# Value products behind the neighbour pieces in each attention slot

## The chip, the core and the metric

The kernel runs on one core of one Trainium2 chip. The metric is device time in microseconds (us) of one execution. The core's engines are named as in the profile: PE is TensorE, which multiplies; PEld is its loading of weights; DVE is VectorE; ACT is ScalarE; POOL is GpSimd; SP issues transfers. Each engine works through its own queue in order, and they wait for each other with semaphores.

## What is computed

The input is 8 batches of 256 tokens of width 512, in 32-bit floats. Four layers follow each other, each as `x = x + layernorm(layer(layernorm(x)))`: a state-space mixer with an MLP, a LoRA MLP, an attention layer, and a linear layer with table-coded weights. The change lies in the attention layer, which the kernel fuses with the last one:

```
qkv = x @ w_qkv                                  # 32 query heads, 8 key/value heads of width 16
xq, xk = rope(xq), rope(xk)
scores = where(causal, xq @ xk.T * scale, -inf)  # per head, 256 x 256
out = softmax(scores) @ values                   # values repeated over 4 query heads
y = out @ w_o
...
x = x + layernorm(y)
x = x + layernorm(layernorm(x) @ w.T + bias)     # the last layer
```

## The kernel before, in words

`attention_layer` walks through the 8 batches in slots, 24 to a batch (`UNITS`). A slot belongs to one unit of attention: a key/value head g and a part r, where r = 0 is the first 128 query rows of four query heads and r = 1, 2 are the second 128 rows of two heads each. The work of a unit is spread over several slots, and every engine has its own loop over the slots:

- `scores(u)` on PE (L1762 to L1769): query times key, then the mask as one more product with an identity matrix. It is issued one slot ahead.
- `maximum(u)` on DVE (L1695): the negated row maximum of the scores, `t_nmax`.
- `exponentials(u)` on ACT (L1573): the probabilities `t_p`.
- `transposes(u)` on PE (L1776): four transposes of the probabilities.
- `high(u)` on ACT (L1566) and `low(u)` on DVE (L1701) take the transposed probabilities out of PSUM as two halves, `t_pT_hi` and `t_pT_lo`, whose sum has the full precision.
- `values(u)` on PE (L1791, L1792 for r = 0; L1797, L1798 for r = 1, 2): values times the two halves, into `OT`. It is issued two slots late, and waits for `pl`, that is for `low(u)`.

Beside this, each slot carries pieces of the neighbouring batches, written out by hand in `JOBS_AT`: the turn of the normalised input (`x`, `a`, `h`: four PE transposes, L1830), the projections (`qq`, `kv`, `o`, `l`: products through the helper `product`, L115 to L117), the stacked transposes that make the query and key tiles (`q`, `k`, L1843), and the transposes of the finished attention output (`back`, L1836). They share two PSUM banks in turn, and `bank_read` waits until the piece that had the bank before has been read out.

What the other engines do for the pieces stands at fixed places of their loops. In its slot s, DVE first drains the pieces that PE ended in slot s - 1 (`drain`), then takes `maximum(s + 1)`, then `turned_low` (L1687), which makes `t_hT_lo`, the low half of a turned input, then `low(s - 1)`, then the statistics of the layernorms. ACT drains the pieces first (`t_hT_hi` L1513, `t_qT` L1523, `t_kT` L1528, `t_v` L1534, `t_oT` L1561), then `high(s - 1)`, then `exponentials(s + 1)`. POOL makes the stacks two slots ahead (L1430, L1432).

A projection needs both halves of its turned input. Below, slot numbers are those within a batch. In four places a piece follows the slot in which its input, or the input that had its bank, was turned: slot 7 (`qq` after `x` in slot 6), slot 10 (`o`, whose bank the turn `a` of slot 9 had), slot 19 (`l` after `h` in slot 18) and slot 22 (`l` after `h` in slot 21). The table lines of these:

```
    (("qq", 0, 1, 1),),                      # slot 7
    (("back", 0, 0, 0), ("o", 0, 0, -1)),    # slot 10
    (("back", 1, 0, 0), ("l", 0, 0, -1)),    # slot 19
    (("l", 0, 1, -1),),                      # slot 22
```

Of the kernel before, what the change touches and what calls it, by code (L numbers as in the profile page):

```python
# [112 lines left out]
def product(pe, out, w_hi, w_lo, x_hi, x_lo, first, last):  # L113

    pe.matmul(out, w_hi, x_hi, start=first, stop=False)  # L115
    pe.matmul(out, w_hi, x_lo, start=False, stop=False)  # L116
    return pe.matmul(out, w_lo, x_hi, start=False, stop=last)  # L117
# [1111 lines left out]
SLOTS = BATCH * UNITS  # L1229
# [34 lines left out]
def name_of(what, part, tile, batch):  # L1264

    return (what, tile, batch) if what in HALVED else (what, part, tile, batch)
# [40 lines left out]
def attention_layer(nc, d, consts, stream, w_hi, w_lo, l_hi, l_lo, bias, keep):  # L1307
# [10 lines left out]
    with ExitStack() as ctx:  # L1318
# [48 lines left out]
        def wait(eng, sem, value):  # L1367
            if value > 0:
                eng.wait_ge(sem, value)
# [10 lines left out]
        def bank_of(job):  # L1380
            return ps[:, X + BANK_OF[job], :]
# [367 lines left out]
        def _(pe):  # L1749
            def scores(u):  # L1750
                b, g, r = u // UNITS, u % UNITS // 3, u % 3
                wait(pe, ex, u - 1)
                if u % UNITS == 0:
                    pe.wait_ge(st_out, max(STACKED["q", 0, 1, b], STACKED["k", 0, 1, b]))
                elif u % 6 == 0:
                    pe.wait_ge(st_out, STACKED["q", g // 2, 1, b])
                    if g == 4:
                        pe.wait_ge(st_out, STACKED["k", 1, 1, b])
                bank = ps[:, S + u % 2, :]
                if r == 0:  # L1760
                    for h in range(2):
                        pe.matmul(bank[:, 2 * h * P:2 * (h + 1) * P].rearrange("p (h t) -> p h t", h=2),  # L1762
                                  qT[:, 2 * g + h, 0:P], kT[:, :, g, 0:P], start=h == 0, stop=False)
                    pe.matmul(bank.rearrange("p (h t) -> p h t", h=4), id_r[:, :],  # L1764
                              mask[:, :].unsqueeze(1).broadcast_to([P, 4, P]), start=False, stop=True).then_inc(sc, 1)
                else:
                    pe.matmul(bank.rearrange("p (h t) -> p h t", h=2), qT[:, 2 * g + r - 1, P:SEQ], kT[:, :, g, :],
                              start=True, stop=False)
                    pe.matmul(bank.rearrange("p (h t) -> p h t", h=2)[:, :, P:SEQ], id_r[:, :],  # L1769
                              mask[:, :].unsqueeze(1).broadcast_to([P, 2, P]), start=False, stop=True).then_inc(sc, 1)  # L1770
# [8 lines left out]
            def values(u):  # L1779
                b, g, r = u // UNITS, u % UNITS // 3, u % 3  # L1780
                part, j = g // 3, g % 3
                s = min(r, 1)
                pe.wait_ge(pl, u + 1)
                if u % UNITS == 0:
                    pe.wait_ge(vl, 2 * b + 2)
                fresh, final = j == 0 and r < 2, j == TRIPLES[part][1] - 1 and r != 1
                if fresh:
                    wait(pe, oe[s], 3 * b + part)
                v = lambda t: v2[:, b % 2, t, g * V_STEP - j * HD:g * V_STEP - j * HD + P]
                if r == 0:  # L1790
                    pe.matmul(ps[:, OT, :], v(0), pT_hi[:, u % 2, :], start=fresh, stop=False)  # L1791
                    mm = pe.matmul(ps[:, OT, :], v(0), pT_lo[:, u % 2, :], start=False, stop=final)  # L1792
                else:
                    out = ps[:, OT + 1, (r - 1) * SEQ:r * SEQ].rearrange("p (h n) -> p h n", h=2)
                    of = lambda part, t: part[:, u % 2, :].rearrange("p (h t n) -> p h t n", h=2, t=2)[:, :, t, :]
                    for t in range(2):
                        pe.matmul(out, v(t), of(pT_hi, t), start=fresh and t == 0, stop=False)  # L1797
                        mm = pe.matmul(out, v(t), of(pT_lo, t), start=False, stop=final and t == 1)  # L1798
                mm.then_inc(pv, 1)

            def bank_read(job):

                if job is None:
                    return
                what, t, b = job[0], job[-2], job[-1]
                i = tile(t, b)
                if what in ("x", "a", "h"):
                    pe.wait_ge(tl, TURN[what, t, b] + 1)
                elif what in ("q", "k"):
                    pe.wait_ge(st_out, STACKED[job])  # L1810
                elif what == "back":
                    pe.wait_ge(osm, BACK[job[1], t, b] + 1)
                elif what == "qq":
                    pe.wait_ge(straight, 2 * i + 1)
                elif what == "kv":
                    pe.wait_ge(vl, i + 1)
                elif what == "o":
                    pe.wait_ge(y_out, i + 1)
                elif what == "l":
                    pe.wait_ge(y_biased, i + 1)  # L1820

            def turn(what, t, b, bank):
                if what == "a":
                    pe.wait_ge(on, BACK[2, t, b] + 1)
                    src = ao[:, t, :]
                else:
                    pe.wait_ge(xn if what == "x" else hn, tile(t, b) + 1)
                    src = xf[:, t, :]
                for k in range(DT):
                    mm = pe.transpose(bank[:, k * P:(k + 1) * P], src[:, k * P:(k + 1) * P], ident)  # L1830
                mm.then_inc(x_mm, 1)

            def back(part, s, b, bank):
                pe.wait_ge(oe[s], 3 * b + part + 1)
                for h in range(4):
                    mm = pe.transpose(bank[:, h * P:(h + 1) * P], oT[:, s, h * P:(h + 1) * P], ident)  # L1836
                mm.then_inc(x_mm, 1)

            def stack(what, part, t, b, bank):
                n = STACKED[what, part, t, b] - 1  # L1840
                pe.wait_ge(st_lo, n + 1)
                for k in range(4):
                    mm = pe.transpose(bank[:, k * P:(k + 1) * P], f(stacks[:, n % STACKS, k * P:(k + 1) * P]), ident)  # L1843
                mm.then_inc(x_mm, 1)

            def project(what, part, t, b, bank):
                h = TURN[{"qq": "x", "kv": "x", "o": "a", "l": "h"}[what], t, b]
                pe.wait_ge(tl, h + 1)
                weights = (l_hi, l_lo) if what == "l" else (w_hi, w_lo)
                ks_ = range(DT) if what == "kv" else range(2 * part, 2 * part + 2)  # L1850
                for k in ks_:
                    chunk, cols = k, slice(0, 512)
                    if what == "kv":
                        chunk, cols = 4 + k // 2, slice(k % 2 * 256, k % 2 * 256 + 256)
                    elif what == "o":
                        chunk = 6 + k
                    out = bank[:, 0:256] if what == "kv" else bank
                    mm = product(pe, out, hT_hi[:, h % 3, k, :], hT_lo[:, h % 3, k, :],
                                 weights[0][:, chunk, cols], weights[1][:, chunk, cols], k == 0, k == DT - 1)
                if what == "kv" or part:  # L1860
                    mm.then_inc(x_mm, 1)
# [3 lines left out]
            for s in range(FIRST_SLOT, END_SLOT):  # L1865
                if 0 <= s + 1 < SLOTS:
                    scores(s + 1)
                if 0 <= s - 2 < SLOTS:
                    values(s - 2)
                for what, part, t, b in JOBS[s]:  # L1870
                    job = name_of(what, part, t, b)
                    if what not in HALVED or part == 0:
                        bank_read(BEFORE[job])
                    if what in ("x", "a", "h"):
                        turn(what, t, b, bank_of(job))
                    elif what == "back":
                        back(part, t, b, bank_of(job))
                    elif what in ("q", "k"):
                        stack(what, part, t, b, bank_of(job))
                    else:  # L1880
                        project(what, part, t, b, bank_of(job))
                if 0 <= s < SLOTS:
                    transposes(s)

# [561 lines left out]
```

## Time and profile before

| what | us |
|---|---|
| median of 3 runs | 2055.51 |
| lowest and highest of them | 2047.91, 2056.07 |
| the profiled execution, its own time | 2053.45 |
| its span, first to last instruction | 2051.7 |
| PE busy | 1735.1 (85%) |
| DVE busy | 1079.3 (53%) |
| ACT busy | 771.0 (38%) |
| POOL busy | 566.7 (28%) |

The profiled execution took 1.75 us more than its span, and lies 2.06 us under the median. The span has the mixer first, then the MLPs, and from about 1420 us to its end the attention layer with the last layer. Busy shares are means over these stages.

### The profile page before, as it was taken

The numbers are of one execution on the slowest core, as the hardware profiler recorded it, in microseconds if no ns is written. First come the engines' busy times: TensorE is split into PE (matmuls) and PEld (weight loads), VectorE is DVE, ScalarE is ACT, GpSimd is POOL, SyncE is SP. The second block draws the span as 40 slices with busy tenths as digits, with TensorE's granted clock in tenths as the row PEclk, the third lists the DMA queues.
The fourth block names the chain that finished last, engine by engine and source line by source line (L and its number), as shares of the span: only waits on it lengthen the run. The fifth ranks groups of instructions, "written<-read, shape, count | busy, mean of one in ns | idle before, by whom it ended". The sixth has DMA issues, their size and how long they took to land. (4 is left out here: it accounts for less than half of the span.)

```text
span 2051.7 us, 25546 instructions
## 1 busy us (share of the span) xinstructions
PE 1735.1 (85%) x8557; PEld 1427.0 (70%) x8557; DVE 1079.3 (53%) x2022; ACT 771.0 (38%) x1552; POOL 566.7 (28%) x740
## 2 busy tenths in 40 slices
PE   2888888869999999999999999902898998898884
PEld 2666666647888888877787888702677777787773
DVE  3656565654322322267434333475577677677673
ACT  2415141423212221122222221140687667677770
POOL 0222222231111111144111112412425334443522
PEclk9968686869999999999999999955999999999997
DMA  3000000011000110032101110120000000000000
GB/s 129 1 21 0 20 0 0 0 34 49 26 21 23 32 36 22 29 111 66 48 22 37 31 31 11 42 81 0 1 1 12 1 12 12 1 11 12 6 6 22
DMA packets 28469, 52.20 MB, mean 25 GB/s; under 512 B 3456, under 2 KB 4640, under 8 KB 28352
## 3 DMA queue, kind: packets, MB, share of 16 engines
q1 hardware_dynamic: 28352, 50.73, 7.9%
q8 instruction: 63, 1.03, 0.2%
q14 instruction: 54, 0.44, 0.1%
HBM read 42.33 MB, written 8.39 MB: 25 GB/s over the span
## 5 line engine op out<-in xcount | busy, mean ns | idle before, releaser
L115 PE MATMUL m_ps<-m_hT_hi,m_w_hi 128*128 128x512 f32 x800 | 317.4, 397 | 7.6 <-DVE m_w_lo L1098 5.3
L1116 DVE TENSOR_TENSOR m_prod<-m_prod,m_ps 128x512 f32<-128x512 f32 x100 | 68.8, 688 | 481.7 <-ACT m_prod L996 481.6
L117 PE MATMUL m_ps<-m_hT_hi,m_w_lo 128*128 128x512 f32 x800 | 316.8, 396 | 0.0
L116 PE MATMUL m_ps<-m_hT_lo,m_w_hi 128*128 128x512 f32 x800 | 316.6, 396 | 0.0
L942 POOL TENSOR_TENSOR m_a_lo<-m_prod,m_a_hi 128x512 fp32r<-128x512 f32 x100 | 130.9, 1309 | 640.0 <-ACT m_a_hi L1000 639.9
L996 ACT ACTIVATE m_prod<-m_ps 128x512 f32<-128x512 f32 x100 | 59.7, 597 | 578.5 <-PE m_ps L117 578.5
L1573 ACT ACTIVATE t_p<-t_ps,t_nmax 128x128 f32<-128x128 f32 (+1 forms) x512 | 181.4, 425 | 75.3 <-DVE t_nmax L1695 74.9
L1695 DVE TENSOR_REDUCE t_nmax<-t_ps 128x2 f32<-128x512 f32 (+1 forms) x192 | 132.0, 688 | 96.0 <-PE t_ps L1764 59.3
L115 PEld LDWEIGHTS m_ps<-m_hT_hi,m_w_hi 128*128 128x128 f32 x800 | 150.9, 189 | 44.0 <-issue 5.7
L117 PEld LDWEIGHTS m_ps<-m_hT_hi,m_w_lo 128*128 128x128 f32 x800 | 150.8, 189 | 36.4
L116 PEld LDWEIGHTS m_ps<-m_hT_lo,m_w_hi 128*128 128x128 f32 x800 | 150.9, 189 | 36.2
L115 PE MATMUL m_ps<-m_w_hi,m_a_hi 128*128 128x512 f32 x400 | 158.2, 396 | 0.7 <-POOL m_a_lo L942 0.7
L116 PE MATMUL m_ps<-m_w_lo,m_a_hi 128*128 128x512 f32 x400 | 156.3, 391 | 0.0
L117 PE MATMUL m_ps<-m_w_hi,m_a_lo 128*128 128x512 f32 x400 | 156.0, 390 | 0.0
L1701 DVE TENSOR_TENSOR t_pT_lo<-t_ps,t_pT_hi 128x512 fp32r<-128x512 f32 x192 | 131.3, 684 | 33.1 <-ACT t_pT_hi L1566 32.5
L1566 ACT ACTIVATE t_pT_hi<-t_ps 128x512 fp32r<-128x512 f32 x192 | 116.3, 606 | 61.3 <-PE t_ps L1776 60.8
L1776 PE MATMUL t_ps<-consts,t_p 128*128 128x128 f32 x768 | 115.2, 272 | 1.9 <-ACT t_p L1573 1.9
L1776 PEld LDWEIGHTS t_ps<-consts,t_p 128*128 128x128 f32 x768 | 91.7, 141 | 10.9 <-ACT t_p L1573 2.1
L1051 DVE TENSOR_TENSOR stream<-m_ps,stream 128x512 f32<-128x512 f32 x128 | 79.5, 684 | 31.4 <-PE m_ps L117 31.4
L1000 ACT ACTIVATE m_a_hi<-m_prod 128x512 fp32r<-128x512 f32 x100 | 63.3, 633 | 75.5 <-DVE m_prod L1116 75.5
L115 PEld LDWEIGHTS m_ps<-m_w_hi,m_a_hi 128*128 128x128 f32 x400 | 75.2, 188 | 16.9 <-POOL m_a_lo L942 1.1
L117 PEld LDWEIGHTS m_ps<-m_w_hi,m_a_lo 128*128 128x128 f32 x400 | 75.1, 188 | 16.5
(259 smaller groups left out, 3735.0 us busy)
## 6 DMA issues: line engine op xcount, KB each, us to landing
m_raw<-in_w_mlp SPq DMA_DIRECT2D x75, 256.0 KB, 2.7
a_xt<-in_x SPq DMA_DIRECT2D x4, 1024.0 KB, 5.3
m_old<-in_x SPq DMA_DIRECT2D x16, 256.0 KB, 3.0
x_store<-stream SPq DMA_DIRECT2D x4, 1024.0 KB, 5.1
m_old<-x_store SPq DMA_DIRECT2D x16, 256.0 KB, 2.6
out<-t_yl SPq DMA_DIRECT2D x16, 256.0 KB, 2.0
a_raw<-in_w_mixer SPq DMA_DIRECT2D x14, 256.0 KB, 5.2
q_raw<-in_w_attn SPq DMA_DIRECT2D x10, 256.0 KB, 5.0
```

Of the source, the lines that this page charges most:

```text
L115: pe.matmul(out, w_hi, x_hi, start=first, stop=False)
L116: pe.matmul(out, w_hi, x_lo, start=False, stop=False)
L117: return pe.matmul(out, w_lo, x_hi, start=False, stop=last)
L942: pool.tensor_tensor(a_lo[:, n % 2, :], prod[:, :], f(a_hi[:, n % 2, :]), ALU.subtract).then_inc(lo, 1)
L1000: act.activation(a_hi[:, n % 2, :], prod[:, :], ACT.Copy).then_inc(hi, 1)
L1051: dve.tensor_tensor(tile(i, c), ps[:, ACC + c, :], tile(i, c), ALU.add).then_inc(summed, 1)
L1116: dve.tensor_tensor(prod[:, :], prod[:, :], ps[:, U + TURN_AT["unit", n, 0] % 2, :], ALU.mult).then_inc(prodd, 1)
L1566: act.activation(pT_hi[:, u % 2, :], ps[:, T + u % 2, :], ACT.Copy).then_inc(ph, 1)
L1573: last = act.activation(p[:, u % 2, h * width:(h + 1) * width], ps[:, S + u % 2, h * width:(h + 1) * width], ACT.Exp, bias=nmax[:, u % 3, ...
L1695: dve.tensor_reduce(nmax[:, u % 3, 0:heads], ps[:, S + u % 2, :].rearrange("p (h t) -> p h t", h=heads), AX, ALU.max, negate=True).then_in ...
L1701: dve.tensor_tensor(pT_lo[:, u % 2, :], ps[:, T + u % 2, :], f(pT_hi[:, u % 2, :]), ALU.subtract).then_inc(pl, 1)
L1776: mm = pe.transpose(ps[:, T + u % 2, k * P:(k + 1) * P], p[:, u % 2, k * P:(k + 1) * P], ident)
```

## The change

In PE's loop over the slots the call of `values(s - 2)` moves from before the slot's pieces to behind them. The instructions, their waits and the loops of the other engines stay as they are.

```
             for s in range(FIRST_SLOT, END_SLOT):
                 if 0 <= s + 1 < SLOTS:
                     scores(s + 1)
-                if 0 <= s - 2 < SLOTS:
-                    values(s - 2)
                 for what, part, t, b in JOBS[s]:
...
                     else:
                         project(what, part, t, b, bank_of(job))
+                if 0 <= s - 2 < SLOTS:
+                    values(s - 2)
                 if 0 <= s < SLOTS:
                     transposes(s)
```

## Rows read from the trace of the kernel before

**Rows 1.** The page: busy times, then TensorE's granted clock in 40 slices of the span.

```profile
PE 1735.1 (85%) x8557; PEld 1427.0 (70%) x8557; DVE 1079.3 (53%) x2022; ACT 771.0 (38%) x1552; POOL 566.7 (28%) x740
...
PEclk9968686869999999999999999955999999999997
```

**Rows 2.** Windows, 1724 to 1796 us: busy us of PE, PEld, DVE, ACT, POOL, clock, DMA.

```profile
1724.00:1796.00 72.00, 64.49 (x425) 55.44 (x424) 52.31 (x107) 50.93 (x120) 31.14 (x56) 1.00 0.02 9
```

**Rows 3.** Waits of PE, 1450 to 2006 us: total us, times, longest us.

```profile
PE t_ps L115 <- DVE t_hT_lo L1687: 23.3, 27, 1.5
PE t_ps L1797 <- DVE t_pT_lo L1701: 12.2, 31, 1.0
...
PE t_ps L1791 <- DVE t_pT_lo L1701: 2.4, 3, 1.0
```

**Rows 4.** Timeline: transposes of slot 23, two batches: start us, us, what.

```profile
1652.39 0.60 PE L1776 MATMUL t_ps<-consts,t_p 128*128 128x128 f32 x4
...
1724.56 0.60 PE L1776 MATMUL t_ps<-consts,t_p 128*128 128x128 f32 x4
```

**Rows 5.** Timeline, slot 7: scores, values, the waiting piece on PE; DVE beside it.

```profile
1671.77 0.47 PE L1767 MATMUL t_ps<-t_kT,t_qT 128*128 128x512 f32 x1
...
1672.23 0.39 PE L1797 MATMUL t_ps<-t_pT_hi,t_v 128*128 128x256 f32 x1
1672.39 0.69 DVE L1695 TENSOR_REDUCE t_nmax<-t_ps 128x2 f32<-128x512 f32 x1 [0.22 <-PE t_ps L1769]
...
1673.00 0.68 DVE L1687 TENSOR_TENSOR t_hT_lo<-t_ps,t_hT_hi 128x512 fp32r<-128x512 f32 x1
...
1673.83 0.47 PE L115 MATMUL t_ps<-q_w_hi,t_hT_hi 128*128 128x512 f32 x1 [0.85 <-DVE t_hT_lo L1687]
```

**Rows 6.** Timeline, slot 8: first values product, first product of the piece behind.

```profile
1676.21 0.39 PE L1791 MATMUL t_ps<-t_pT_hi,t_v 128*128 128x512 f32 x1
...
1676.67 0.39 PE L115 MATMUL t_ps<-q_w_hi,t_hT_hi 128*128 128x512 f32 x1
```

**Rows 7.** Timeline, slots 10, 19 and 21 to 22: DVE's maximum, PE's waiting piece.

```profile
1682.63 0.69 DVE L1695 TENSOR_REDUCE t_nmax<-t_ps 128x2 f32<-128x512 f32 x1 [0.16 <-PE t_ps L1769]
...
1683.97 0.51 PE L115 MATMUL t_ps<-q_w_hi,t_hT_hi 128*128 128x512 f32 x1 [0.47 <-DVE t_hT_lo L1687]
...
1709.20 0.69 DVE L1695 TENSOR_REDUCE t_nmax<-t_ps 128x2 f32<-128x512 f32 x1 [0.41 <-PE t_ps L1769]
...
1710.63 0.47 PE L115 MATMUL t_ps<-f_w_hi,t_hT_hi 128*128 128x512 f32 x1 [0.56 <-DVE t_hT_lo L1687]
...
1716.27 0.69 DVE L1695 TENSOR_REDUCE t_nmax<-t_ps 128x2 f32<-128x512 f32 x1 [0.53 <-PE t_ps L1769]
...
1720.33 0.47 PE L115 MATMUL t_ps<-f_w_hi,t_hT_hi 128*128 128x512 f32 x1 [1.49 <-DVE t_hT_lo L1687]
```

**Rows 8.** Timeline, slots 23 to 2: DVE's maximum, the last stacked piece of slot 2.

```profile
1650.73 0.69 DVE L1695 TENSOR_REDUCE t_nmax<-t_ps 128x4 f32<-128x512 f32 x1 [1.26 <-PE t_ps L1764]
...
1660.27 0.63 PE L1843 MATMUL t_ps<-consts,t_stacks 128*128 128x128 f32 x4 [0.58 <-POOL t_stacks L1432]
```

**Rows 9.** Timeline, slots 15, 16 and 18: ACT's key tile, PE's waits.

```profile
1697.28 1.19 ACT L1528 ACTIVATE t_kT<-t_ps 64x512 fp32r<-64x512 f32 x2
1698.52 0.66 PE L1843 MATMUL t_ps<-consts,t_stacks 128*128 128x128 f32 x4 [0.44 <-ACT t_kT L1528]
...
1700.36 0.39 PE L1797 MATMUL t_ps<-t_pT_hi,t_v 128*128 128x256 f32 x1 [0.40 <-DVE t_pT_lo L1701]
...
1707.74 0.63 PE L1830 MATMUL t_ps<-consts,t_xf 128*128 128x128 f32 x4 [0.80 <-DVE t_xf L1619]
```

**Rows 10.** Timeline, slot 9: the low half on DVE, the turn `a` on PE.

```profile
1680.14 0.68 DVE L1687 TENSOR_TENSOR t_hT_lo<-t_ps,t_hT_hi 128x512 fp32r<-128x512 f32 x1
...
1681.20 0.60 PE L1830 MATMUL t_ps<-consts,t_ao 128*128 128x128 f32 x4
```

**Rows 11.** Timeline, first batch before its slots: one 128x512 product.

```profile
1425.48 0.63 PE L117 MATMUL t_ps<-q_w_hi,t_hT_lo 128*128 128x512 f32 x1
```

More of the change, by code:

```diff
@@ L1867, in _ @@
                     scores(s + 1)
-                if 0 <= s - 2 < SLOTS:
-                    values(s - 2)
                 for what, part, t, b in JOBS[s]:
@@ L1881, in _ @@
                         project(what, part, t, b, bank_of(job))
+                if 0 <= s - 2 < SLOTS:
+                    values(s - 2)
                 if 0 <= s < SLOTS:
```

## The prediction

> **What bounds the kernel now.** I read the page first. PE is busy 85% of the span, and its granted clock is full in every slice of the attention stage but those at its two ends [rows 1]. Nothing outside that stage is touched, so the windows of the stage come next. In 72 us of it, just under one batch, PE is busy 64.5 us, DVE 52.3, ACT 50.9 and POOL 31.1, at a granted clock of 1.00 [rows 2]. PE's stream sets the pace, then, and what matters is its 7.5 us of idle time. The waits of PE say what ends it [rows 3]. The largest entry is the first product of a projection waiting for `t_hT_lo`: 27 times, 23.3 us. The waits of the value products for `t_pT_lo` are 34 times, 14.6 us (12.2 + 2.4). The 27 are slots 7, 10, 19 and 22 of six whole batches, slot 7 of the first batch and slots 19 and 22 of the last.
>
> The timeline gives the period: the transposes of slot 23 start 72.17 us apart (1724.56 - 1652.39) [rows 4]. Within a slot the reader is to see what each wait is anchored to. In slot 7, scores start at 1671.77 and the value products at 1672.23. DVE had idled until the scores were there, took the maximum at 1672.39 and `t_hT_lo` at 1673.00, which ends at 1673.68. The piece starts at 1673.83 [rows 5]. The piece therefore waits for a DVE chain that begins with this slot's scores, not with the turn that ended a slot earlier.
>
> **The change, part by part.** No instruction is added or removed. Per slot two (r = 0) or four (r = 1, 2) value products move behind the pieces. Their price is read where nothing waits: from the first value product to the first product of the piece is 0.46 us (1676.67 - 1676.21) [rows 6]. No transfer is issued in this loop, and the queues of DVE, ACT and POOL keep their order.
>
> Where neither a piece nor a value product waits, swapping them costs nothing: the sum on PE is the same, and `transposes(s)` starts when it did.
>
> Where the piece waits and the release is anchored ahead of it, the value products were filling that wait. They now come behind it. The piece starts when it did, PE idles 0.46 us longer ahead of it, and the transposes, the next slot's scores and, through them, DVE's next maximum come 0.46 us later. I go through the places of a steady batch.
>
> - Slot 7: release anchored to the scores at the slot's start, 2.06 us after them (1673.83 - 1671.77) [rows 5]. +0.46.
> - Slots 10 and 19: the same picture. DVE idles for the scores (0.16 and 0.41 us) before the maximum, and the piece starts 1.34 and 1.43 us behind that (1683.97 - 1682.63, 1710.63 - 1709.20) [rows 7]. +0.46 each.
> - Slot 22: DVE last waits for PE at the maximum of slot 21, at 1716.27, and is busy without a gap until the piece starts at 1720.33, 4.06 us later [rows 7]. The anchor is still the scores. +0.46.
> - Slots 0 to 2: DVE last waits for PE at 1650.73, in slot 23, and then runs without a gap through the maximum of slot 2. The last stacked piece of slot 2 starts at 1660.27, on POOL, whose work follows the moments that DVE makes in this stretch [rows 8]. The key tile ahead of slot 1's turn and the 0.19 us that slot 1's value products wait lie inside the stretch and give nothing back. Once for the three slots: +0.46.
> - Slots 14 to 18: the same kind of stretch, through ACT. ACT writes the key tile at 1697.28 because `exponentials(15)` ends there, not because the piece was late, and PE's piece starts at 1698.52. In slot 16 the value products wait to 1700.36, and there the move does give time back, about 0.56 us. But the stretch ends in slot 18 with the turn `h` at 1707.74, behind DVE's normalising [rows 9], and that chain has no PE work in it that moves. What slot 16 gives back is waited off by slot 18. Once for the five slots: +0.46.
> - Slot 9: the turn `a` starts at 1681.20; the low half ahead of it on DVE ends at 1680.82 (1680.14 + 0.68) [rows 10]. The piece would now come 0.46 us earlier, 0.08 us before that. About +0.1 with the semaphore.
>
> A steady batch: 6 x 0.46 + 0.1 = 2.9 us; six of them 17.4 us. The first batch has only slot 7 of these: +0.5. The last has slots 18, 19 and 22: +1.4. These two batches also have slots in which the value products wait and a short `back` or stacked piece could go first (some three places, 0.4 to 0.5 us each): -1.5. Sum: 17.4 + 0.5 + 1.4 - 1.5 = 17.8, say 18 us, all on PE's path.
>
> What I can't read is priced from both sides. From below: all 14.6 us of the value products' waits vanish and no other wait grows. From above: the swap also makes waits where it now starts a piece 0.46 us earlier than its input; with six further places a batch that is 6 x 0.46 x 7 = 19 us more. I stay at 18, since in the rows the anchored waits outnumber the loose ones.
>
> The sum is against the profiled execution, 2053.45 us, and gives 2071.5. The median of the runs is 2.06 us above that execution, so I forecast 2055.5 + 18 = 2073.5, rounded to 2073 us. About 0.5% (10 us) is what a measurement of this kernel can tell from no change.
>
> **The rivals.**
>
> The first ends on the other side: the release moves with the turn. The turn of slot 6, 18 or 21 now ends 0.46 us earlier against its own transposes. If ACT's high half, rather than DVE's maximum, decided when `t_hT_lo` is made, the release would come 0.46 us earlier too, the cover lost would be won back, and the 14.6 us of waits would be gone: 2055.5 - 14.6 = 2041 us. It decides from the point where ACT's high half ends after DVE's maximum. Against it is slot 7, where the maximum followed an idle DVE and `t_hT_lo` started 0.61 us behind its start, directly in the queue [rows 5]. The Trainium skill (Perfetto Trace Analysis, Optimization Strategy) advises to find what a gap waits for and make it start sooner; the change does that to the turns. By this rule, the rival should win; the trace disagrees in slot 7, since what starts sooner isn't the last to arrive.
>
> The second is no change: the waits of the value products vanish (-14.6), and only the four turned inputs of a batch cost, over 27 places: 27 x 0.46 = 12.4. That gives 2053 us. It needs the stretches 0 to 2 and 14 to 18 to pay nothing. For it: slot 16 does give 0.56 us back. Against: slot 18's anchor [rows 9].
>
> The third is more of the same: six further places a batch start to wait, 2073.5 + 19 = 2093 us. For it: slot 9 shows a margin of 0.38 us, less than the 0.46 by which the piece moves [rows 10].
>
> The fourth is the clock. PE's longest wait in these slots, 1.49 us, grows to about 2.0, and the granted clock was 1.00 across all of these waits before [rows 2, 7]. A 128x512 product took 0.63 us at the start of the stage, where the granted clock was at its lower level of 1.2 GHz [rows 11], against 0.39 in slot 8 [rows 6]. If the clock fell once a batch and 10 such products ran at that length, seven batches would pay 7 x 10 x 0.24 = 17 us, which makes 2090 us. The Trainium skill (TensorE: Matmul & The Clock Gate, Why this matters for your kernels) warns of idle gaps in the middle of a kernel for this reason; no row of this stage shows such a fall.
>
> **How the numbers follow.** The forecast gets 0.70. The release that moves with the turn gets 0.06, no change 0.12, more of the same 0.09, the clock 0.03. The range has to reach past the forecast's own error: the last batches' guesses (1.5 us), the spread of the runs (8 us) and half of the third rival's extra places (10 us). That makes 2061 to 2085. The forecast, the third and the fourth rival are all slower by over 0.5% (above 2066): 0.82. The first is faster: 0.06. The second is within 0.5%: 0.12.
>
> **What would show it.** In the waits of PE, the entry for `t_hT_lo` should grow by about 27 x 0.46 = 12 us, to 36; the value products' waits should fall from 14.6 to under 4; and the waits of stacked pieces for the key tile should grow by about 0.46 us each. The period should go from 72.17 to 75.1 us. In slot 7 the piece should still start about 2.06 us behind the scores, with the value products behind it. The prediction is wrong if that distance shrinks, if slots 14 to 18 come out no longer than before, or if the value products still wait.

## The result, and the profile after

The changed kernel takes 2081.17 us (median of 4 runs, 2078.32 to 2082.16) against 2055.16 (4 runs, 2047.91 to 2056.07): ratio 1.0132 [1.0107, 1.0157], so 26 us or 1.3% slower. Run again later beside other runs of the kernel before, it took 2075.78 us (2071.70 to 2083.21), ratio 1.0098 [1.0071, 1.0124]. I had forecast 2073, in 2061 to 2085, with 0.82 for slower.

The page of the kernel after, the lines that answer to [rows 1]: the same instructions and the same busy time of PE (1735.7 us against 1735.1), in a span of 2080.4 us instead of 2051.7.

```profile
PE 1735.7 (83%) x8557; PEld 1432.9 (69%) x8557; DVE 1078.3 (52%) x2022; ACT 772.1 (37%) x1552; POOL 566.6 (27%) x740
...
PEclk9978686879999999999999999956999999999996
```

So the time is idle time of PE. The windows of the kernel after, the same 72 us as in [rows 2]: PE is busy 62.12 us of them instead of 64.49, at the same granted clock.

```profile
1724.00:1796.00 72.00, 62.12 (x415) 54.18 (x414) 49.53 (x101) 48.49 (x114) 30.08 (x54) 1.00 0.02 8
```

The waits of PE after, 1450 to 2036 us (total us, times, longest us), against [rows 3].

```profile
PE t_ps L115 <- DVE t_hT_lo L1687: 38.5, 28, 2.0
PE t_ps L1843 <- ACT t_kT L1528: 15.0, 14, 1.5
...
PE t_ps L1830 <- ACT t_kT L1528: 6.6, 6, 1.4
...
PE t_ps L1797 <- DVE t_pT_lo L1701: 1.9, 5, 0.5
...
PE t_ps L1791 <- DVE t_pT_lo L1701: 1.0, 1, 1.0
```

The waits for `t_hT_lo` grew from 23.3 to 38.5 us; those of the value products fell from 14.6 to 2.9. They were not saved: they stand now in front of the pieces, for the turned inputs and also for ACT's key tile (`t_kT`), where the stacked pieces (L1843) waited 6.8 us before and the turns (L1830) 0.9.

The timeline of the kernel after (start us, us, engine, operation; in brackets the idle time before it and what ended it). First slot 7, against [rows 5]; then the stacked pieces of slot 15, against [rows 9]; those of slot 17; the turn of slot 18, against [rows 9]; slot 22, against [rows 7]; and the transposes of slot 23, two batches, against [rows 4].

```profile
1686.31 0.48 PE L1767 MATMUL t_ps<-t_kT,t_qT 128*128 128x512 f32 x1
...
1686.94 0.69 DVE L1695 TENSOR_REDUCE t_nmax<-t_ps 128x2 f32<-128x512 f32 x1 [0.37 <-PE t_ps L1769]
...
1687.55 0.68 DVE L1687 TENSOR_TENSOR t_hT_lo<-t_ps,t_hT_hi 128x512 fp32r<-128x512 f32 x1
...
1688.38 0.47 PE L115 MATMUL t_ps<-q_w_hi,t_hT_hi 128*128 128x512 f32 x1 [1.47 <-DVE t_hT_lo L1687]
...
1689.85 0.28 PE L1797 MATMUL t_ps<-t_pT_hi,t_v 128*128 128x256 f32 x1
...
1714.11 0.66 PE L1843 MATMUL t_ps<-consts,t_stacks 128*128 128x128 f32 x4 [0.90 <-ACT t_kT L1528]
...
1719.94 0.65 PE L1843 MATMUL t_ps<-consts,t_stacks 128*128 128x128 f32 x4 [1.47 <-ACT t_kT L1528]
...
1723.33 0.63 PE L1830 MATMUL t_ps<-consts,t_xf 128*128 128x128 f32 x4 [1.48 <-DVE t_xf L1619]
...
1736.86 0.47 PE L115 MATMUL t_ps<-f_w_hi,t_hT_hi 128*128 128x512 f32 x1 [1.96 <-DVE t_hT_lo L1687]
...
1741.57 0.60 PE L1776 MATMUL t_ps<-consts,t_p 128*128 128x128 f32 x4
...
1816.67 0.60 PE L1776 MATMUL t_ps<-consts,t_p 128*128 128x128 f32 x4
```

In slot 7 the piece starts 2.07 us behind the scores (1688.38 - 1686.31), as before (2.06), with DVE's maximum and low half at the same distances; PE stands idle for 1.47 us of it instead of 0.85, and the value products follow. Between two batches now lie 75.10 us (1816.67 - 1741.57) instead of 72.17.

Two of the waits for the key tile have no row above. The first two lines are the kernel before, the turn `x` of slot 1 and the stacked piece of slot 17; the last is the kernel after, the turn `x` of slot 1.

```profile
1656.57 0.66 PE L1830 MATMUL t_ps<-consts,t_xf 128*128 128x128 f32 x4 [0.19 <-ACT t_kT L1528]
...
1704.36 0.66 PE L1843 MATMUL t_ps<-consts,t_stacks 128*128 128x128 f32 x4 [0.63 <-ACT t_kT L1528]
```

```profile
1745.75 0.66 PE L1830 MATMUL t_ps<-consts,t_xf 128*128 128x128 f32 x4 [1.08 <-ACT t_kT L1528]
```

Slot by slot (from transposes to transposes, after minus before, in a batch at full clock), the steps are +0.46 in slots 1, 7, 15, 19 and 22, +0.48 in slot 10, +0.16 in slot 9, -0.46 in slot 16 and +0.44 in slot 17. All others are within 0.03. Together +2.9 us. In slot 1 it is the turn `x` that loses its cover: its wait for the key tile is 1.08 us instead of 0.19.

**Where the rest of the 28.7 us of the span is.** From the transposes of slot 0 in the first batch (1454.05 us before, 1458.63 after) to the last transposes (2000.21, 2028.86) the slots take 546.16 and 570.23 us: +24.1. The other 4.6 us lie ahead of all slots, in code that did not change; over all profiles here that point lies anywhere from 1449 to 1459 us, at 1456.46 for the same changed kernel run again. Of the 24.1, six whole batches at +2.93 are 17.6, the first batch is +0.3 and the last +2.8. The remaining 3.4 us are in the first two of the six, which took 77.25 and 77.52 us (72.45 and 72.99 before, so 1.87 and 1.60 over +2.93). The windows of the kernel after show what sets them apart (busy us of PE, PEld, DVE, ACT, POOL, granted clock, DMA). The first covers the 3.86 us up to the end of a `t_hT_lo` wait of slot 22, the next two what follows it, the fourth the stretch behind such a wait a batch later. The fifth has one of the other four such waits in it, and the last is slots 18 and 19 of the last batch.

```profile
1579.00:1582.86 3.86, 1.89 (x17) 1.60 (x15) 3.76 (x9) 2.56 (x7) 1.60 (x4) 1.00 0.00 0
1582.86:1586.21 3.35, 3.35 (x11) 2.77 (x12) 1.23 (x3) 0.12 (x1) 0.69 (x2) 0.54 0.00 0
1586.21:1590.00 3.79, 3.79 (x23) 3.32 (x23) 2.44 (x5) 2.41 (x7) 0.70 (x1) 0.96 0.00 0
...
1660.36:1664.98 4.62, 4.62 (x18) 4.13 (x19) 1.39 (x4) 0.72 (x2) 0.69 (x2) 0.63 0.00 0
...
1732.00:1740.00 8.00, 6.04 (x43) 5.34 (x42) 5.34 (x13) 3.94 (x9) 2.29 (x5) 1.00 0.00 0
...
2009.50:2013.00 3.50, 2.97 (x13) 2.96 (x14) 1.58 (x3) 1.67 (x5) 1.36 (x4) 0.54 0.00 0
```

Behind the wait that ended at 1582.86 the granted clock is 0.54, most of the way to the lower level of 1.2 GHz, and behind the one that ended at 1660.36 it is 0.63. Behind the equal wait at 1736.86 it stays at 1.00. In the last batch it is 0.54 from 2009.50 on, and that fall is not behind slot 22: PE's wait there is a shorter one, of the turn `h` in slot 18.

```profile
2010.03 1.09 PE L1830 MATMUL t_ps<-consts,t_xf 128*128 128x128 f32 x4 [1.52 <-DVE t_xf L1619]
```

The slots of the kernel before have no such fall:

```profile
1470.00:2000.00 530.00, 473.36 (x3109) 405.66 (x3108) 384.87 (x766) 381.25 (x903) 213.27 (x388) 1.00 0.02 7
```

The last batch's +2.8 contains some 1.5 us of it (slots 18 and 19 are +2.4, where two places at 0.46 are 0.9). So the slots cost about 19 us by the order and about 5 by the clock.

### The profile page after: what moved, and what is told of

Read it like the earlier page. It is cut to its first block and busy times, and to the rows that moved or that the text cites. A ratio compares the mean times of both kernels' runs of the same rounds, so it can differ in the third digit from the quotient of the medians.

```text
span 2080.4 us, 25546 instructions
## 1 busy us (share of the span) xinstructions
PE 1735.7 (83%) x8557; PEld 1432.9 (69%) x8557; DVE 1078.3 (52%) x2022; ACT 772.1 (37%) x1552; POOL 566.6 (27%) x740
## 5 line engine op out<-in xcount | busy, mean ns | idle before, releaser
L115 PE MATMUL t_ps<-q_w_hi,t_hT_hi 128*128 128x512 f32 (+1 forms) x192 | 72.8, 379 | 21.1 <-DVE t_hT_lo L1687 21.1
```

## The experiments

"Ratio" is against runs of the kernel before on the same chip. "Period" is the distance of equal transposes in two batches at full clock: 72.16 before, 75.10 after.

**Which slots cost.** Three kernels in which the value products come behind the pieces in some slots only. The edit, for a set `BEHIND` of slots of a batch (the pieces stand at the line of dots):

```
                if 0 <= s - 2 < SLOTS and not BEHIND(s % UNITS):
                    values(s - 2)
...
                if 0 <= s - 2 < SLOTS and BEHIND(s % UNITS):
                    values(s - 2)
```

In the first, slots 7, 10, 19 and 22 alone.

> Value products behind the pieces only in slots 7, 10, 19 and 22, where a piece waits for a turned input; ahead of them in all other slots. Theory A (the wait's release is anchored to the slot's own scores, so the value products lose their cover): 27 places x 0.46 us = +12.4 us on the kernel before, about 2067.5 us; the period of a batch goes from 72.17 to 74.0 us; each fall of the clock behind a longer wait adds 1 to 2 us. Rival B (the loss of the changed kernel lies elsewhere, in the clock and in the waits for banks): within 2 us of before, period 72.2.

Measured: 2074.75 us, ratio 1.0077 [1.0040, 1.0115], period 74.01. The steps in the four slots are +0.47 each, and no other slot changes. Two of the batches took 75.6 instead, again with a low clock behind slot 22. So four places alone are 1.85 us a batch, as in the sum. The median lies 7 us over the 2067.5 that I had expected: the runs spread over 14 us (2063.68 to 2077.24), and the profiled one has three falls of the clock, two in whole batches and one behind slot 22 of the last.

In the second, all slots but those four.

> The complement: value products behind the pieces in all slots but 7, 10, 19 and 22. Theory A: the stretches 0 to 2 and 14 to 18 cost 0.46 us each and slot 9 0.15, so the period is 72.17 + 1.07 = 73.2 us and the time is 6 us over before, about 2061 us. A rival by which only the turned inputs cost: period 72.2 or below, time 2050 to 2055 us, since the value products' own 14.6 us of waits are won back.

Measured: 2063.46 us, ratio 1.0033 [1.0016, 1.0049], period 73.26. The steps are slot 1 +0.45, slot 9 +0.16, slot 15 +0.47, slot 16 -0.47, slot 17 +0.45. Both long stretches pay once, and slot 16's gift of 0.47 is taken back in slot 17. The second rival (no change), which needed them to pay nothing, falls here: 73.26 against 72.17. The waits of PE in this kernel, 1450 to 1960 us, show the key tile as the largest after the turned inputs, where the kernel before had 6.8 us for it (L1688 and L1844 of this kernel are L1687 and L1843, moved down a line by the edit).

```profile
PE t_ps L115 <- DVE t_hT_lo L1688: 22.2, 25, 1.5
...
PE t_ps L1844 <- ACT t_kT L1529: 15.0, 14, 1.5
```

The third has only the slots for which the prediction names no anchored wait (3 to 6, 8, 11 to 13, 20, 21, 23).

> Value products behind the pieces only in the slots in which neither kind waits in a steady batch (3 to 6, 8, 11 to 13, 20, 21, 23). Theory A: the swap alone is free, period 72.17 us, time within 1.5 us of before (the first and the last batch may win up to 1.5). Rival (the swap itself costs, by the order of the weight loads or by pieces that now start ahead of their input): period 72.5 or more, time 2058 us or more.

Measured: 2059.51 us, ratio 1.0012 [0.9995, 1.0028], period 72.53 and not 72.17. All of the +0.39 is in slot 3, where the piece now right behind the scores is `back`. The timeline of this kernel, slot 3: ACT's key tile, then PE.

```profile
1737.13 1.19 ACT L1529 ACTIVATE t_kT<-t_ps 64x512 fp32r<-64x512 f32 x2
...
1738.38 0.66 PE L1837 MATMUL t_ps<-consts,t_oT 128*128 128x128 f32 x4
1739.00 0.50 PE L115 MATMUL t_ps<-q_w_hi,t_hT_hi 128*128 128x512 f32 x1
```

`back` starts 0.06 us behind the end of the key tile (1738.32); in three other batches the records name the key tile as what `back` waits for. From the transposes of slot 2 to `back` that is 0.89 us (1738.38 - 1737.49), where the value products started 0.78 behind them before: 0.11. The four transposes then take 0.62 us to the next product where they took 0.35 before, and why isn't shown. A slot that I had counted as loose is not, if the slots ahead of it run at their old speed. In the changed kernel it costs nothing (+0.00), since PE comes to it 0.46 us later anyway.

With slot 3 taken out of the set, one run:

> Value products behind the pieces only in slots 4 to 6, 8, 11 to 13, 20, 21 and 23. In the run that had slot 3 too, the period was 72.53 us, and 0.39 us of it came up in slot 3, where the piece waits for the key tile. Theory A: without it the swap is free and the period is 72.17 us. Rival (the swap has a price of its own): 72.5 us.

Measured: 2054.17 us, period 72.16, no step in any slot of a steady batch. Where neither neighbour waits, the swap is free.

**Is it the cover?** Of each slot's value products one half ahead of the pieces, one half behind (the pieces stand at the line of dots):

```
                if 0 <= s - 2 < SLOTS:
                    values(s - 2, (0,))
...
                if 0 <= s - 2 < SLOTS:
                    values(s - 2, (1,))
```

> Half of each slot's value products stay ahead of the pieces, the other half goes behind them. Theory A: the price is the duration of what was moved, so each place costs 0.23 us in place of 0.46: period 72.17 + 1.4 = 73.6 us, time about 13 us over before, 2068 us. Rival (one product behind the piece is enough, since what counts is which comes last): period 75.1 us, time as with the whole change, 2081 us.

Measured: 2065.91 us, ratio 1.0039 [1.0025, 1.0053], period 73.64: half of the 2.94. The steps are +0.23 to +0.26 in slots 7, 10, 15, 17, 19, 22, -0.23 in slot 16 and +0.19 in slot 1. With none, half and all of the value products moved, the cost is in proportion to the PE time taken from in front of the wait. The clock did not fall in the slots.

**Could the release move with the turn?** The first rival. In the changed kernel the low half of the turned input goes ahead of the next maximum on DVE:

```
+                turned_low(s)
                 if 0 <= s + 1 < SLOTS:
                     maximum(s + 1)
-                turned_low(s)
```

> The changed kernel, with DVE's low half of a turned input taken before the maximum in each slot. Theory A (in slots 10, 19 and 22 the maximum stands ahead of the low half and anchors the release to the scores): the wait falls by about 0.6 us in slots 10 and 22 and 0.2 in slot 19, and by nothing in slot 7, where ACT's high half ends just as the maximum does; 1.4 us a batch, some 10 us in all, about 2071 us. Rival (ACT's high half decides in all four): no change, 2081 us, and the waits stay at 0.94, 1.03 and 1.96 us.

Measured: 2065.69 us, ratio 1.0054 [1.0038, 1.0071], period 72.88, 2.2 us under the changed kernel where I had expected 1.4. The timeline of this kernel, slot 10:

```profile
1681.12 0.60 ACT L1513 ACTIVATE t_hT_hi<-t_ps 128x512 fp32r<-128x512 f32 x1
...
1681.83 0.68 DVE L1687 TENSOR_TENSOR t_hT_lo<-t_ps,t_hT_hi 128x512 fp32r<-128x512 f32 x1
1682.18 0.60 PE L1836 MATMUL t_ps<-consts,t_oT 128*128 128x128 f32 x4
1682.42 0.68 DVE L1695 TENSOR_REDUCE t_nmax<-t_ps 128x2 f32<-128x512 f32 x1
1682.56 0.50 PE L115 MATMUL t_ps<-q_w_hi,t_hT_hi 128*128 128x512 f32 x1
```

The low half starts when ACT's high half has ended, and the product waits for nothing. Against before, slot 10 is now 0.68 us shorter, slot 19 0.24 and slot 22 0.14; slots 7 and 3 still pay 0.30 and 0.52. Once DVE's queue puts nothing anchored to the scores ahead of the low half, the release does move with the turn. By the next run, which has the low half first and the value products in their old place, that is shown for slots 10 and 19 (-0.68 and -0.24 here, -0.66 and -0.22 there); slot 22 still pays its full 0.46 (-0.14 here, -0.60 there). The clock fell twice in the last batch.

The same edit in the kernel before:

> The kernel before, with DVE's low half of a turned input taken before the maximum in each slot. Theory A: slot 10's wait of 0.47 us goes, slot 19's falls by 0.2, slot 22's by 0.6, slot 7's stays at 0.85: 1.3 us a batch, some 9 us in all, about 2046 us. Rival (the later maximum makes the exponentials and the transposes late, or ACT's high half decides): 2055 us or above.

Measured: 2052.60 us, ratio 0.9978 [0.9960, 0.9996], period 71.17, 1.0 us less than before instead of 1.3. Slots 10, 19 and 22 give 0.66, 0.22 and 0.60; slot 3 takes 0.51 back.

And without slot 2, whose low half had pushed slot 3's maximum back:

```
+                if s % UNITS != 2:
+                    turned_low(s)
                 if 0 <= s + 1 < SLOTS:
                     maximum(s + 1)
-                turned_low(s)
+                if s % UNITS == 2:
+                    turned_low(s)
```

> The kernel before, with the low half ahead of the maximum in all slots but slot 2 of a batch. The run with it in all slots won 0.66, 0.22 and 0.60 us in slots 10, 19 and 22 and lost 0.51 in slot 3. Theory A: the loss comes from slot 2, where the maximum, the exponentials and behind them the key tile became late, so without it the period is 72.17 - 1.48 = 70.7 us, and the time 72.17 - 70.7 = 1.5 us a batch below before, some 10 us, about 2046 us. Rival (the loss in slot 3 has another origin): period 71.2 us, 2052 us.

Measured: 2048.14 us, ratio 0.9960 [0.9944, 0.9975], period 70.67.

Then the four turned slots of the change put on this kernel:

> The best version so far (period 70.67 us) with the value products behind the pieces in slots 7, 10, 19 and 22. With the maximum ahead of the low half this cost 4 x 0.46 us a batch (period 74.01 against 72.17). Theory A: where ACT's high half decides when the low half is made, the release moves with the turn, which ends 0.46 us earlier if the value products of its own slot are behind it. But here the turns stand in slots 6, 9, 18 and 21, whose value products stay ahead, so nothing is won back: 4 x 0.46, period 72.5 us. Rival (the place of the value products in the waiting slot does not matter once the low half goes first): period 70.7 to 71.4 us.

Measured: 2064.73 us, ratio 1.0039 [1.0022, 1.0056], period 72.56: slots 7, 10, 19 and 22 pay +0.48, +0.50, +0.46 and +0.48 over the kernel without them. The waits of PE, 1500 to 1940 us, are 12.6 us for `t_hT_lo` without the move, and with it:

```profile
PE t_ps L115 <- DVE t_hT_lo L1687: 20.5, 17, 1.5
```

So with the low half first, the four places still cost their full price when `values` moves in these slots alone, for then the turn a slot earlier does not come sooner. With all slots moved, slots 10 and 19 paid nothing over the kernel with the low half first alone (-0.68 and -0.24 against -0.66 and -0.22). So it takes the move in other slots to win their cover back; that these are slots 9 and 18, where the turns stand, follows from the code, but no run moves those alone. The last batch has one fall of the clock here, behind a wait of 2.02 us in its slot 10.

**The clock.** The changed kernel once more, unchanged:

> The changed kernel once more, as it is. Theory A: the period is 75.1 us again and the sum over the slots again 20 us or so; the time at which the attention slots begin differs from the first profile by up to 4 us, since nothing ahead of them was changed, and the clock falls to its lower level for a stretch behind some of the waits of slot 22, but not behind the same ones. Rival (both belong to the changed program): the same beginning and the same falls.

Measured: 2075.78 us (2083.21, 2075.03, 2076.52, 2071.70), periods of 75.12 to 75.14 at full clock, and 77.20, 77.54 and 76.37 in the first three batches. The windows of this run behind the waits in slot 22:

```profile
1582.00:1585.00 3.00, 3.00 (x15) 2.74 (x14) 0.00 (x0) 0.30 (x1) 0.00 (x0) 0.60 0.00 0
1661.00:1664.00 3.00, 3.00 (x13) 2.57 (x12) 1.63 (x3) 1.50 (x5) 0.00 (x0) 0.68 0.00 0
1737.00:1740.00 3.00, 3.00 (x17) 2.69 (x16) 0.94 (x2) 0.81 (x2) 0.00 (x0) 0.83 0.00 0
```

The last batch has two falls more, in slot 2 and behind slot 22. The order costs the same in both runs; in how many batches the clock falls varies.

The changed kernel with only slot 22 put back:

> Value products behind the pieces in all slots but slot 22. Theory A: period 75.1 - 0.46 = 74.64 us. If the falls of the clock come from the longest wait (1.96 us in slot 22), there are none between 1470 and 2010 us, and the time is some 3 us (the slots) plus 2 to 3 us (the clock) under the whole change, about 2075 us. Rival (the clock falls for another reason): falls as before and 2078 us.

Measured: 2076.39 us (2068.31 to 2078.13), ratio 1.0110 [1.0084, 1.0136], period 74.66. The windows of this run, the whole batches and then one place in the last batch:

```profile
1570.00:1700.00 130.00, 112.46 (x747) 98.15 (x746) 92.46 (x189) 87.25 (x207) 54.35 (x96) 1.00 0.03 9
1700.00:1955.00 255.00, 215.92 (x1438) 187.83 (x1438) 177.81 (x357) 175.99 (x412) 104.98 (x191) 1.00 0.02 8
1960.00:1964.00 4.00, 4.00 (x22) 3.67 (x21) 1.69 (x4) 3.01 (x7) 1.80 (x5) 0.62 0.19 70
```

No whole batch has a fall from 1570 us on, where the two runs with slot 22 changed had two and three. I had expected none in the last batch either, and there is one, in slot 2, behind two waits that are shorter than many without a fall:

```profile
1957.65 0.63 PE L1844 MATMUL t_ps<-consts,t_stacks 128*128 128x128 f32 x4 [0.93 <-POOL t_stacks L1433]
1959.06 0.63 PE L1844 MATMUL t_ps<-consts,t_stacks 128*128 128x128 f32 x4 [0.78 <-POOL t_stacks L1433]
```

In its profiled run the slots take 563.79 us, 6.4 less than in the changed kernel's; seven places at 0.46 are 3.2 of it, and the rest, about 3, is left for the clock. The median doesn't show that gain: its interval and that of the changed kernel's second set overlap, so by the time alone the case for the clock isn't made; it rests on the granted clock in the profiled runs.

**A version that beats both.** In the kernel with the low half first but in slot 2, slot 22 still waits 0.89 us for `t_hT_lo`, behind DVE's moments of slot 21. Those, and the roots on POOL that follow, go one slot later:

```
-                if n == 21 and in_batch(b - 1):
+                if n == 22 and in_batch(b - 1):
```

> The best version so far (low half ahead of the maximum but in slot 2, period 70.67 us), and the moments of the last layer's first tile go from slot 21 to slot 22 on DVE, their roots on POOL likewise. Theory A (in slot 22 DVE's queue, busy since slot 21, sets the release): DVE reaches the low half 0.8 us earlier, but ACT's high half ends only 0.2 to 0.3 us before the present start, so the wait of slot 22 falls by 0.2 to 0.5 us: period 70.2 to 70.5 us, about 2046 us. Rival (ACT's high half alone decides there by now, or the later roots hold up POOL and the addition): period 70.7 us or more.

Measured: 2045.22 us (2043.95 to 2045.80), ratio 0.9940 [0.9924, 0.9957], period 70.25, slot 22 another 0.53 us shorter, slot 1 0.09 longer. Its `t_hT_lo` waits, 1500 to 1940 us, are 9.4 us against 20.4 in the kernel before in that window:

```profile
PE t_ps L115 <- DVE t_hT_lo L1687: 9.4, 18, 0.8
```

## Why the prediction came out right, and what it missed

**The steady batch: right.** 2.94 us measured, 2.9 predicted, and each of the seven terms in its slot: the four turned inputs at 0.46 to 0.48, the stretches 0 to 2 and 14 to 18 once each, slot 9 at 0.16. Shown by the parts: four slots alone +1.85, the others alone +1.10, together 2.95; half of the move, half of the cost; the swap in loose slots free.

**The anchor in slot 7: right.** The distance from scores to piece stayed at 2.07 us.

**The stretch through slot 16: right.** The value products there gave 0.46 back (I had put it at 0.56), and it was waited off in slot 17, whose wait for the key tile went from 0.63 us to 1.47. I had put the end of the stretch at slot 18; the steps put it one slot earlier.

**What should show: it did.** `t_hT_lo` waits 38.5 us (36 forecast; the 28th is slot 10 of the last batch), value products 2.9 (under 4), slot 15's key tile wait 0.44 to 0.90, period 75.10. The waits for the key tile in slots 1 and 17 grew by more than the 0.46 that I had named, by 0.89 and 0.84; part of that is the 0.19 and 0.40 us that the value products of slots 1 and 16 had waited before.

**First batch and last: the net about right, the parts not.** +0.3 and, the clock left out, +1.3, against +0.5, +1.4 and -1.5 for both together. Slot by slot, the places where time comes back give about 3 us and not 1.5: slots 12, 16, 18 and 19 of the first batch 0.45 to 0.6 each, slots 4 and 15 of the last 0.67 and 0.31. But places that I had not counted pay: slots 2, 14, 15 and 17 of the first batch 0.2 to 0.6 each, slots 2 and 10 of the last 0.45 each. The net is +1.6 instead of +0.4; that it is no further off is luck, since the two errors cancel in part. The slots without the clock are 19.2 us (17.6 + 1.6) instead of 17.8.

**The first rival** does not happen in this kernel, and the order of DVE's queue is why in slots 10 and 19: with the low half ahead of the maximum it happens there. In slot 22 it does not happen even so, where DVE's moments of slot 21 still stand ahead. My condition for it, ACT's high half against DVE's maximum, compares the right two operations, but I had looked at it in slot 7 alone.

**The third rival** is wrong for the changed kernel: no further place of a steady batch pays. The one loose place that can, slot 3, does so only when slots 0 to 2 are left as they were.

**The fourth rival was under-priced in chance and over-priced in size.** I gave 0.03 to a clock that falls behind slot 22. It does fall there, in two of six whole batches and in three of six, at 1.2 to 1.9 us each, and in the last batch elsewhere too (once in the run shown, some 1.5 us): about 5 us in the run shown where I had worked out 17. I had read a granted clock of 1.00 across waits of up to 1.49 us as evidence for a wait of 2.0, and it is not. Nor is the length of one wait what decides: in the last batch falls came around waits of 1.52 us and behind 0.93 and 0.78 us. The forecast and a part of this rival held together; I had set them up as alternatives. The Trainium skill (TensorE: Matmul & The Clock Gate, Why this matters for your kernels) warns of idle gaps in the middle of a kernel, longer ones than any in these slots. The traces agree in that the falls in whole batches come behind the waits of 1.95 to 1.98 us in slot 22 and nowhere else, and go beyond it in that gaps this short can have a fall behind them, if not most times: 7 of 18 such waits in the three profiled runs that have them.

**The size in all: 18 us forecast, 26.0 measured in the first comparison, 19.0 in the second.** So it was too low by 8 and by 1. In the profiled run, against the sum's 17.8, the first and last batches are 1.2 us of it, the clock 4.9, and the scatter ahead of the slots, where no code changed, 4.6. That scatter seems to be most of the runs' spread as well: the three profiled runs in which the slots began earliest, at 1449 to 1450 us, lie 7 to 8 us under the medians of their kernels (2058.87 under 2065.69, 2040.53 under 2048.14, 2068.31 under 2076.39). How much of the medians' difference it makes stays open, since only profiled runs can be taken apart.

## What to carry to other kernels

Work that stands in front of an anchored wait is free; moved behind it, it costs its full duration once for each anchored stretch, however many waits the stretch has, unless what ends the wait moves with it. So follow each wait through the releasing engine's queue to the last place where that engine itself was idle: if it waited there for something that your change does not start sooner, the release stays. If a release is late because of its place in an in-order queue, change that order first: here it was worth 0.4% (0.6% with the moments moved as well), while changing PE's order lost 1.3%.

## What the runs showed of the hardware

In the middle of a stage that keeps PE busy 62.12 of 72 us, the granted clock can fall behind a wait of under 2 us: it was 0.54 over the 3.35 us behind the wait of 1.97 us ending at 1582.86, and 1.00 behind an equal wait at 1736.86 and, by the period of 75.10 us, in the three batches that follow. The same kernel had two falls in one profiled run and three in another. In whole batches nothing fell where the longest wait was 1.7 us (half of the products moved) or 1.8 us (all slots but the four, all but slot 22, and the low half first, each in slot 18 of one batch). In last batches there were falls around a wait of 1.52 us and behind two of 0.93 and 0.78 us, the latter with slot 22 unchanged. So the length of a single wait doesn't tell a wait with a fall from one without, and what does is open.
